# New order of the first loads and of the work where two stages meet, and unread matrix products in TensorE's first gaps

## The reference, cut to what matters

```
att  = softmax(gelu(gelu(c @ W0 + b0) @ W1 + b1) @ W2 + b2)        # 32 x 8
y    = einsum('boi,bih->boh', einsum('bk,koi->boi', att, weight), x) + att @ bias_k
r    = softmax(y @ gate_w.T)                                        # 2048 x 8
x1   = x + ((y * (r @ in_scale)) @ sign(weight).T) * (r @ out_scale) + bias

z    = grouped_conv1d(x1, 9 taps, 4 groups) + c @ c_weight.T + fside
res  = z @ W.T + b
w    = softmax over 8 experts of (sum(q * k) / sqrt(32)),  q, k = z @ Wq.T, z @ Wk.T
out  = x1 + res + einsum(w, z @ A, Bm)
```

## Time and profile before

| | |
|---|---|
| median of 3 runs | 557.45 us (555.99 to 559.61) |
| the profiled execution | 560.03 us, of which the span from the first to the last instruction 558.0 |
| busy share: PE, DVE, POOL, ACT | 97%, 46%, 28%, 22% |
| mean granted clock of TensorE | 0.991 of full |
| one tile in the middle of stage one | 10.1 us |
| one tile in the middle of stage two | 22.5 us |

### The profile page before, as it was taken

One profiled execution on the slowest core, in us unless ns is written; L12 is line 12 of the kernel. 1 busy time (PEld: TensorE's weight loads), 2 busy tenths in 40 slices (PEclk: granted clock), 3 DMA queues, 4 the chain that ended last, 5 costly groups with the idle time before them and its releaser, 6 DMA issues.

```text
span 558.0 us, 13990 instructions
## 1 busy us (share of the span) xinstructions
PE 538.6 (97%) x5717; PEld 461.9 (83%) x5717; DVE 254.7 (46%) x461; ACT 123.4 (22%) x289; POOL 155.5 (28%) x79
## 2 busy tenths in 40 slices
PE   5879999999999899999999999999999999999997
PEld 4657788787887798898988988989889899898896
DVE  4439888797775762323224332242232322422321
ACT  5614434343434320101101011011011110110100
POOL 0027776767758490110101101011011010110100
PEclk9989999999999989999999999999999999999999
DMA  8684565555558451330412303204033032130100
GB/s 311 241 330 159 172 204 187 197 197 187 204 172 215 132 185 43 81 104 17 119 51 66 117 14 103 95 22 118 38 80 113 4 118 78 40 118 39 39 39 38
DMA packets 38775, 66.79 MB, mean 120 GB/s; under 512 B 4384, under 2 KB 25056, under 8 KB 38752
## 3 DMA queue, kind: packets, MB, share of 16 engines
q1 hardware_dynamic: 38528, 66.09, 36.3%
q10 hardware_dynamic: 224, 0.36, 0.3%
HBM read 49.64 MB, written 16.79 MB: 119 GB/s over the span
## 4 chain that ended last, share of the span: by engine, by line
PE 92%; DVE 3%; DMA 2%; ACT 1%; issue 1%; SPq 0%; DVEq 0%; ACTq 0%
PE bank L587 52%; PE bank L491 19%; PE bank L566 8%; PE bank L622 4%; PE bank L425 3%; DMA xs<-in_x 2%; PE bank L438 2%; PE bank L467 2%; DVE parts L912 1%; DMA cst<-in_consts 1%; ACT late L693 1%; PE bank L448 0%; PE bank L455 0%; PE bank L473 0%; ACT parts L724 0%
## 5 line engine op out<-in xcount | busy, mean ns | idle before, releaser
L587 PE MATMUL bank<-early,parts 128*128 128x320 f32 (+1 forms) x1152 | 208.2, 339 | 1.8 <-DVE parts L912 1.8
L587 PEld LDWEIGHTS bank<-early,parts 128*128 128x128 f32 x1152 | 186.1, 189 | 18.7 <-issue 2.2
L491 PE MATMUL bank<-late,parts 128*128 128x512 f32 x512 | 131.1, 408 | 1.5 <-ACT parts L724 1.5
L1101 POOL TENSOR_TENSOR work<-work,bias_bc 128x1024 f32<-128x1024 f32 x16 | 38.0, 2375 | 279.2 <-DMA work<-x_scratch 279.2
L491 PEld LDWEIGHTS bank<-late,parts 128*128 128x128 f32 x512 | 95.0, 193 | 22.6 <-ACT parts L724 1.7
L587 PE MATMUL bank<-late,parts 128*128 128x512 f32 x384 | 94.1, 394 | 0.0
L587 PEld LDWEIGHTS bank<-late,parts 128*128 128x128 f32 x384 | 70.9, 188 | 15.9
L912 DVE TENSOR_TENSOR parts<-y_t,parts 128x512 fp32r<-128x512 f32 x64 | 59.4, 931 | 12.3 <-ACT parts L724 11.0
L724 ACT ACTIVATE parts<-y_t 128x512 fp32r<-128x512 f32 x64 | 39.7, 633 | 98.7 <-DVE y_t L995 67.0
L1066 POOL TENSOR_TENSOR work<-work 128x512 f32<-128x512 f32 x32 | 45.9, 1436 | 49.4 <-DVE work L920 48.2
L1016 DVE TENSOR_TENSOR qk<-bank,qk 128x256 f32<-128x256 f32 x16 | 6.8, 425 | 104.6 <-ACT qk L810 104.6
(11 more groups left out here) (91 smaller groups left out, 351.0 us busy)
## 6 DMA issues: line engine op xcount, KB each, us to landing
xs<-in_x SPq DMA_DIRECT2D x16, 512.0 KB, 3.4
work<-in_x SPq DMA_DIRECT2D x16, 512.0 KB, 3.3
x_scratch<-work SPq DMA_DIRECT2D x16, 512.0 KB, 3.0
raw<-x_scratch SPq DMA_DIRECT2D x128, 64.0 KB, 3.0
work<-x_scratch SPq DMA_DIRECT2D x16, 512.0 KB, 3.7
out_tokens<-work SPq DMA_DIRECT2D x15, 512.0 KB, 2.7
stage<-in_wearly SPq DMA_DIRECT2D x8, 576.0 KB, 3.9
row_bc<-token_rows_scratch SPq DMA_DIRECT2D x30, 64.0 KB, 3.2
```

What stands on the lines that cost most here:

```text
L491: last = mm(bank[4 + h][:, :], parts[:, p, a, c, :], signs[:, c, h * HALF:(h + 1) * HALF], start=(k % 16 == 0), stop=(k % 16 == 15))
L587: return mm(dst, parts[:, p, a, c, :], w(b, c), start=(k == 0), stop=(close and k == 23))
L1101: g.tensor_tensor(resid[:, p, :], resid[:, p, :], bias_bc[:, :], ALU.add).then_inc(resid_ready, 1)
```

## The change

- **First loads.** Behind the load for tile (1, 0), SP now issues the broadcast of the bias and the load for tile (1, 1), and only then the two reloads of `resid`.
- **Unread products.** TensorE multiplies a cleared buffer (`weighted`) and the constants at five places of the first 20 us; nobody reads the results, which go to bank 4. VectorE clears the buffer first, and one new wait keeps the bank's earlier content until it is copied.
- **Where the stages meet.** The first convolution stands at step 4 in place of 8 of the last tile; the eight gathers for it move ahead of a store, a reload and more on SP; ScalarE rounds z of tile (0, 0) ahead of its last work for stage one; GpSimd waits for both rests of z before it splits the last chunk, and then adds the last bias; TensorE begins stage two with seven chunks ready and waits for the eighth at product 21.

```diff
-TURN_AT, BLOCK_AT, SUM_AT, CONV0_AT = 7, 18, 26, 8
+TURN_AT, BLOCK_AT, SUM_AT, CONV0_AT = 7, 18, 26, 4
...
+            sp.wait_ge(scale_ready, 1)
+            sp.dma_start(bias_bc[:, :], bias0.broadcast_to([P, H])).then_inc(bias0_loaded, 16)
+            load_next(1, 1, 4)
             for p in range(2):
                 sp.wait_ge(signs_ready, 7 + p)
                 load_again(0, p)
-            sp.wait_ge(scale_ready, 1)
-            sp.dma_start(bias_bc[:, :], bias0.broadcast_to([P, H])).then_inc(bias0_loaded, 16)
-            load_next(1, 1, 4)
...
+            load_next(last, 1, 4 * late_i + 8)
             sp.wait_ge(pads_zeroed, 2)
             load_raw(0, 0)
+            replace_x1(late_i, 0)
...
+            def keep_busy(operand, *columns):
+
+                for n in columns:
+                    mm(bank[4][:, 0:n], operand[:, 0:P], operand[:, 0:n], start=True, stop=True)
+
+            pe.wait_ge(idle_operand_cleared, 1)
+            keep_busy(weighted[:, :, :].rearrange("p s k -> p (s k)"), HALF, P)
...
+            keep_busy(cst, 2 * P)
             pe.wait_ge(consts_loaded[2], 16)
+            keep_busy(cst, 2 * P)
...
+            keep_busy(cst, P // 2)
             first_rows(0)
...
             first_rows(1)
+            pe.wait_ge(first_rows_ready, 1)
+            keep_busy(cst, P)
...
             turn_routing(0, 0, True)
+            keep_busy(cst, P, P)
...
+                        if late_ready and h == 0 and k == 21:
+
+                            pe.wait_ge(stage_hi[0], 8)
+                            pe.wait_ge(stage_lo[0], 8)
...
-            pe.wait_ge(stage_hi[0], 8)
-            pe.wait_ge(stage_lo[0], 8)
+            pe.wait_ge(stage_hi[0], 7)
+            pe.wait_ge(stage_lo[0], 7)
...
-            period0(last, 1, None, None, last)
-
             act.wait_ge(ffn0_done, 2 * TILES - 2)
             round_parts(0, 0, z_t, z_biased, z_hi, by_token)
+            period0(last, 1, None, None, last)
...
+            v.memset(weighted[:, :, :], 0.0).then_inc(idle_operand_cleared, 1)
...
+            period0((last - 1, 1), (last, 0))
+            make_x1(last, 0, 1)
+            pool.wait_ge(z_lo, 2)
+            split_chunk(last)
+            add_bias0(last, 1)
+            make_x1(last, 1, 0)
             make_x1(last, 1, 1)
```

More of the change, by code:

```diff
@@ L126, in adaln_ffn_kernel @@
         bank = [ctx.enter_context(nc.psum_tensor(f"bank{k}", [P, HALF], F32)) for k in range(8)]
+        idle_operand_cleared = sem("idle_operand_cleared")
         consts_loaded = [sem(f"consts_loaded{k}") for k in range(3)]
@@ L308, in _, with load_raw @@
             late_i, last = PAIRS - 3, PAIRS - 1
+            def load_raw(i, p):
+                sp.wait_ge(x1_stored[p], 16 * (i + 1))
+                src = tile_rows(x1_dram, 2 * i + p).rearrange("(n c) (l q) -> l c n q", c=CG, l=L8)
+                half = L8 // 2
+                for lo in range(2):
+                    for l in range(half):
+                        part = (lo * half + l) * CG
+                        at = 1 - lo
+                        sp.dma_start(raw[part:part + CG, p, :, at:at + P],
+                                     src[(1 - lo) * half + l]).then_inc(raw_loaded[p], 16)
             load_next(last, 1, 4 * late_i + 8)
+            sp.wait_ge(pads_zeroed, 2)
+            load_raw(0, 0)
             replace_x1(late_i, 0)
@@ L325, in _ @@
             next_chunk(last - 1)
[L327 to L340, removed]
             load_raw(0, 1)
@@ L1070, in rest_of_stage, with split_chunk @@
                 g.tensor_tensor(dst, stage[:, p, 0:n], hi.bitcast(F32), ALU.subtract).then_inc(stage_lo[p], 1)
+            def split_chunk(chunk):
+                hi, lo = (early[:, a, bass.ds(chunk, 1), :].rearrange("p a n -> p (a n)") for a in range(2))
+                rest_of_stage(0, NW, chunk + 1, lo, hi)
             def period0(before, now, chunk=None):
@@ L1077, in period0 @@
                 if chunk is not None:
-                    hi, lo = (early[:, a, bass.ds(chunk, 1), :].rearrange("p a n -> p (a n)") for a in range(2))
-                    rest_of_stage(0, NW, chunk + 1, lo, hi)
+                    split_chunk(chunk)
                 make_x1(*now, 0)
@@ L1087, in _ @@
             rest_of_stage(1, H, 1, lora[:, 1, :], lora[:, 0, :])
-            with pool.Fori(1, PAIRS) as i:
+            with pool.Fori(1, PAIRS - 1) as i:
                 period0((i - 1, 1), (i, 0))
```

## The result

Over 7 executions each, side by side, the changed kernel has a median of 552.66 us (551.57 to 554.29) and the kernel before 557.16 us. The ratio is 0.9926 with a 95% interval of 0.9904 to 0.9947: 4.5 us faster by the medians. The forecast was 547.8 us, the range 543.5 to 551.6. The time lies above the range: faster as forecast, but by 4.5 us in place of 9.65.

A forecast was written before the change was run, and what follows sets the result against it. TensorE bounds the kernel, so only its gaps and low-clock stretches pay: 4.13 + 3.35 - 0.7 - 0.7 = 6.1 us at the start plus 3.5 at the junction, 9.6. So 560.03 becomes 550.4, less 2.58 is 547.8 us; range 543.5 to 551.6.

The forecast's parts named there:

- The sum's last step: Going from the profiled execution to the median: its 2.58 us offset above 557.45 kept, so 550.4 becomes 547.8 us.
- the two terms: Costs at the start: L858 slowed beside GpSimd, 0.7 us (0 to 1.5); unread products on the path, 0.7 (0.3 to 1.2).
- The wait of 4.13 us: TensorE's idling before L438 at 35.31 for `xs` of tile (1,1); the earlier load was to remove all of it.
- the 0.7 for L858: VectorE's L858 for tile (1,1), delayed beside GpSimd's earlier L1059, would make TensorE's L438 0.7 us late.
- The half clock: 6.83 us at 0.51 of full clock from 36.37, behind the wait for `xs`; its removal was to save 3.35 us.
- What is late next: After the first loads: GpSimd starts L1059 near 28 us and may slow VectorE's L858, a cost of 0.7 us.
- Rival (a): Unread products raise the clock before the first L491, saving a further 3.0 us: 544.8 us, chance 0.24.
- The junction: Where the stages meet: earlier `z_lo` removes 1.84 us of idling and 1.67 of lower clock, 3.5 us.
- Covers: Slack for moved work: 2.4 us for chunk 7's split before product 21, 0.4 us for the `resid` reload behind the gathers.
- (b): At the start, the load of `xs` is still late: 1.5 us of wait, 1.7 of low clock; 551.0 us, chance 0.12.
- (c): Where the stages meet, `z_lo` stays late or chunk 7 takes its place: 3.5 us lost, 551.3 us, chance 0.08.
- (d): Gathers put ahead on SP starve GpSimd of the `resid` reload: slower than before, about 559 us, chance 0.04.

The follow-up runs named there:

- e1: The kernel before, run and profiled again with no edit: 556.67 us, ratio 1.0005.
- e2: The kernel before with only the new order of the first loads: 553.68 us against 556.84.
- e7: The changed kernel with ScalarE's copy of the next logits ahead of its rounding of chunk 0 in tile (0,1): 553.00 us against 556.90 before.
- e4: The changed kernel without the unread products, their clearing and their wait: 551.14 us against 556.84 before.
- e5: The kernel before with only the unread products, their clearing and their wait added: 558.55 us against 556.90.
- e6: The changed kernel, run and profiled again with no edit: 551.51 us against 556.90 before.
- e3: The kernel before with only the new order where the stages meet, no new first loads or unread products: 554.25 us against 556.84.
- e11: The changed kernel without unread products and with GpSimd's old order at the end of stage one: 550.97 us against 557.67 before.
- e12: The kernel before with ten unread 128-column products in TensorE's wait for `xs` of tile (1,1): 554.97 us against 557.67.
- e9: The changed kernel with only three unread products, in the 1.48 us gap before the first 128x512 product: 550.73 us against 557.67 before.
- e8: The changed kernel without unread products and with ScalarE's logits copy ahead of its chunk 0 rounding: 551.07 us against 556.90 before.

## Why the prediction was wrong

- **The sum's last step failed: "That execution is 2.58 above the median ... and I leave the offset as it is".** The profiled execution stood above the median because it had lost more clock (0.991 against 0.994) and, as far as two profiles tell, waited longer. The sum had taken these same losses out already, and taking the gain from the median's 557.45 as well counted them twice. Without this step the sum is 550.4. The best execution of the changed kernel had 550.8, the middle one of 13 had 552.3.
- **The error of 4.9 us in parts.** 2.6 are this step. 1.2 lie in the profile, 551.57 for 550.4, all of it ahead of the end of stage one. The last 1.1 are the distance of the median, 552.66, from the profiled execution, which was the fastest of its seven. Three of the seven have a clock of 0.996 or 0.997; for the rest of it the cause stays open.
- **Bounds.** I wrote of "2.6 if the median's run had less of the clock's loss than the profiled one", and yet set the forecast at the far end of it and the range's upper end at 551.6. That case was the usual one. The bounds were also added wrongly: 0.8 and 0.5 us up from the two terms, and 2.6, reach 551.7 and not 551. The measured time is above either.
- **The first loads** were right in kind, and near in size partly by luck: on the profiles 5.8 us up to the transpose against 6.1 forecast. The wait of 4.13 us went, the 0.7 for L858 did not come, and the stretch from L438 to the transpose took 1.1 us longer than at full clock in e1, 0.8 of it the stop at 33.66 that nobody foresaw. The half clock was the mis-sized term: taken at 3.35, measured 2.2, since 0.9 comes back as a wait before the end of stage one (e1). So 4.9 us are left at the end of stage one. And both the wait and the clock were taken from one execution: in e1 they are 2.85 us and nothing. By the median the whole edit is 3.2 us (e2).
- **What is late next** was looked for at the wrong engine. VectorE's L858 behind GpSimd (0.7) didn't occur, since the reload of `resid` reached GpSimd at 32.05 and not near 28; so nothing here tests what the two engines would have cost each other at this place. What came was a wait of 1.46 us at 45.09 for ScalarE's copy, behind its rounding of chunk 0. The kernel before stops at the same product when its clock is full, for 0.87 us in e1. e7 shows that this rounding isn't the end of it: the chain from the routing holds TensorE at the next transpose.
- **The unread products** cost about 1.2 us (e4, e5; the pairs give 0.4 to 1.9) where I took 0.7 from 0.3 to 1.2. Rival (a) is refuted in size: the first L502 did run at full clock in the changed kernel's profile, and it bought none of the 3.0 us, because ScalarE's copy at 26.60 held the place; in e6 an earlier rise bought 0.4. I had the row of that copy and used it only to lower the figure.
- **The junction** gave 3.4 us between the profiles (the changed kernel is 4.9 us ahead at the end of stage one, and 8.3 behind the 48 products of 128x320, 195.98 for 204.32), forecast 3.5, and 2.6 by the median (e3). The mechanism of VectorE's rests was right, the edit named for it wasn't (e11). The eighth chunk was a second holder at the same place (e2); I counted its later wait as a risk, and it was also part of the gain. Covers held: nothing waited at product 21.
- **Rivals (b), (c), (d)** did not happen: no wait for `xs`, no wait at product 21, and the reload behind the gathers was in time.

## What to carry to other kernels

When a profile shows stretches at a lower clock behind a wait, ask first in how many executions they are there: compare the mean granted clock and the time of several executions, and take the gain from the median's clock, never from the profiled execution and then again by its distance to the median. Ask also whether another engine would hold TensorE right behind the stretch: part of the time at half clock is then hidden already. Products that nobody reads kept the clock in the long wait of the kernel before (e12); the same in a short gap brought no gain that the runs show (e9), and those ahead of a place that another engine's queue sets put the real work off (e5). Undo each part of a reordering by itself: here GpSimd's new order, to which I had given the junction's gain, could be undone at no cost (e11), and leaving the unread products out gives a kernel (e4, e8, e11, 551.0 to 551.1 us) that is below the changed one.

## What the runs showed of the hardware

- The same instructions with the same data differ by 1.3% between executions (553.84 to 560.97 us), and most of it follows the granted clock (the table in e1).
- Idling and the clock behind it, at the wait for `xs`: 4.13 us (before) was followed by 6.8 us at half clock, 4.53 (e3) and 3.17 (e5) by some 3.4 us each, 2.85 (e1) by none. At the junction: 1.84 us (before) and 2.02 (e2) by some 3.4 us, 1.10 (e1), 1.89 (e12) and 2.01 (e5) by none. Filling the wait for `xs` kept the clock (e12). So the length of the idling alone doesn't tell whether the clock falls.
- The clock's column reads 1.00 from the start of a profile although the first products have the lower level's durations (six L491 in 2.93 us against 1.64 us). Losses there don't show in the mean clock; durations do.
- In both profiles of the changed kernel (33.66 in the one above) and in e7's TensorE stopped for 0.65 to 1.1 us in the middle of 32 small products, with "issue" as the cause and transfers busy at over 0.9. e8's has 0.31 us of it, e2's and e4's none with the transfers just as busy, so these alone don't make it. The three with the long stop have the new loads and all unread products; whether that is the cause, nothing that was run tells.
